# TensorE's loop over the tiles: eight steps in an iteration instead of four

## Chip, cores and metric

The kernel runs on one core of one Trainium2 chip. The metric is the device time of one execution in microseconds (us); the kernel before takes 488.36 us (median of 3 runs, 488.33 to 488.38). The engines are TensorE (PE for its matmuls, PEld for its weight loads), VectorE (DVE), ScalarE (ACT), GpSimd (POOL) and SyncE (SP). Each has a sequencer that takes instructions in the program's order, does the scalar ones (register arithmetic, branches, loads of a register) itself and hands the others to its engine.

## The reference

The input is 128 sequences of 64 tokens with 256 values each. Every sequence has two indices: one picks one of 8 experts for a first layer, the other one of 16 domains for a second.

```python
# layer 0, weights picked per sequence by expert_idx (8 experts, H = 256, I = 1024)
h = gelu(einsum('bsh,bhi->bsi', x, Wi[expert_idx]) + bi[expert_idx])
r = einsum('bsi,bih->bsh', h, Wo[expert_idx]) + bo[expert_idx] + x
y = layernorm(r) * gamma[expert_idx] + beta[expert_idx]
# layer 1, an adapter of width 64 with a matrix per domain (16 domains)
hidden = gelu(y @ down_W.T + down_b)
hidden = hidden @ expert_W[domain].T + expert_b[domain] + domain_emb[domain]
out = layernorm(hidden @ up_W.T + up_b + y) * ln_gamma + ln_beta
```

## The kernel before, in words

The host only lays arrays out. On the chip the 128 sequences are first sorted by expert, in pairs: a **tile** is two sequences, 128 tokens, and there are 64 tiles. The first 60 (PURE) have one expert each, the last 4 are mixed. Weights are kept as a high and a low half of 16 bits, so each product is three matmuls (high by high, high by low, low by high).

All engines walk through the same **steps** (`STEPS` = 69), each as a software pipeline of its own, tied to the others by semaphores alone. TensorE's `step` (line 1022) does for step i, in this order:

- the sequencer reads four words of the index table (`indices(pe, 4 * i + IDX_PE, 4, ...)`, the load is recorded at line 274): where the weights of tile i and of tile i - 1 lie and the two domains' tables. With them it works out addresses (`first_addresses`, lines 986 to 992, `second_addresses`, line 994);
- the first product of tile i, 8 columns of 6 matmuls (lines 1006 to 1008, into `p_h`), with the up product of tile i - 4 after the first column (lines 1039 and 1043, into `p_u`) and the down product of tile i - 3 after the third (line 1029, into `p_d`);
- the bias row of tile i - 1 (line 1117) and its second product, 8 times 3 matmuls (lines 1017 to 1019, into `p_o`), with the transposes of tile i - 2 in its middle (line 1051, into `p_t`).

So line 1039 occurs once in each step from step 4 on, and marks the steps in the trace.

`run` (line 288) lays the steps out on an engine: a **lead** written out in full, then a hardware loop (`eng.Fori`, line 292) whose body holds `unroll` steps, and then the rest written out. The loop's own instructions (counter, branch, start value) are recorded at line 294. For TensorE the lead is steps 0 to 5, the loop covers the 48 steps 6 to 53, and steps 54 to 68 follow, written out. `run`'s default is four steps in an iteration. GpSimd (line 562) and TensorE (line 1131) use it; ScalarE (line 693), VectorE (line 911) and SyncE (line 416) pass `NCH` = 8, because their steps name one of eight weight chunks by its place in the body. Of the chunk that `run` hands to a step, TensorE only asks whether there is one.

Of the kernel before, what the change touches and what calls it, by code (L numbers as in the profile page):

```python
# [16 lines left out]
WCH, NCH = 512, 8  # L17
# [31 lines left out]
def build(nc, t):  # L49
# [4 lines left out]
    with ctx:  # L54
# [233 lines left out]
        def run(eng, step, unroll=4, ahead=EARLY, first_looped=LEAD):  # L288

            lead, mid = first_looped - ahead, CHUNKS - FIRST_CHUNKS - ahead  # L290
            for i in range(lead):
                j = i + ahead
                step(i, i % 2, i % 4, (j % NCH, (j + FIRST_CHUNKS) // NCH, j % SLOTS_W))
            with eng.Fori(0, (mid - lead) // unroll) as n:
                i = eng.snap(n * unroll + lead)
                for q in range(unroll):
                    step(i + q, q % 2, (lead + q) % 4,
                         (q, n + (FIRST_CHUNKS + first_looped) // NCH, (first_looped + q) % SLOTS_W))
            for i in range(mid, STEPS):
                step(i, i % 2, i % 4, False)  # L300
# [121 lines left out]
        def _(pool):  # L422
# [79 lines left out]

            def step(i, parity, four, weights):
                e_third, e_before, _, _, e_next = indices(pool, i + (IDX_EXP - 3), 5, E0 - 1)
                if exists(i - 5):

# [407 lines left out]
        def _(pe):  # L914
# [213 lines left out]
                            ins.then_inc(s2_done, 1)  # L1128

            pe.wait_ge(idx_ready, TILE_READY)  # L1130
            run(pe, step)


# [45 lines left out]
```

## Time and profile before

| what | value |
|---|---|
| time, median of 3 runs | 488.36 us (488.33 to 488.38) |
| time of the profiled execution | 488.29 us |
| its span, first to last instruction | 486.5 us |
| busy: PE, PEld, DVE, ACT, POOL | 458.1, 423.3, 341.8, 362.3, 343.7 us |
| granted TensorE clock, mean | 0.98 |
| TensorE's loop, steps 6 to 53 | from about 62 to 384 us of the span |
| steps in an iteration: PE and POOL; DVE, ACT and SP | 4; 8 |

All durations of the trace come from the one profiled execution; its span is 1.8 us shorter than its own time and its time 0.07 us below the median. Times in the trace count from the span's start. PE and PEld are one engine and overlap. A row whose engine has a "q" at its end (PEldq) is of the sequencer: its time isn't counted as busy. A matmul's record begins when it begins to stream, and ends later than the next one begins; so the distance from one start to the next is what a matmul costs, not its recorded length.

### The profile page before, as it was taken

Reading aid. Unit: us, or ns where it says so; the run is one execution under the profiler, and the core shown is the slowest. Engines: PE = TensorE matmul, PEld = TensorE weight load, DVE = VectorE, ACT = ScalarE, POOL = GpSimd, SP = SyncE. Lnnn points to the kernel's source line nnn. Section 1 sums busy time; section 2 is a strip of 40 time slices with the busy share of each in tenths; the row PEclk is TensorE's granted clock in tenths of the full one; section 3 lists DMA queues with packets and bytes.
Section 4 is the critical chain, followed back from the end, with each engine's and each line's share of the span. In section 5 each row is a group of like instructions: output and inputs, shape, how many; then the busy total and the mean of one; then the engine's idle time right before and its main releaser. Section 6 shows DMA issues by size and latency. Waiting matters only on the chain.

```text
span 486.5 us, 18826 instructions
## 1 busy us (share of the span) xinstructions
PE 458.1 (94%) x5724; PEld 423.3 (87%) x5725; DVE 341.8 (70%) x910; ACT 362.3 (74%) x1087; POOL 343.7 (71%) x567
## 2 busy tenths in 40 slices
PE   3599999999999999999999999999999999999972
PEld 2388999999999999999999999999999999888861
DVE  7677777777777777777777787777777766665352
ACT  2499777887777877778877788777787777776631
POOL 5043677887778877887778877887778877754565
PEclk9889999999999999999999999999999999999995
DMA  3924334333333343433433333333332222220001
GB/s 105 333 73 106 95 99 104 104 102 92 98 100 95 103 104 87 99 96 102 104 89 95 102 101 98 86 98 101 101 98 65 60 62 61 62 56 25 26 22 34
DMA packets 66806, 44.33 MB, mean 91 GB/s; under 512 B 41537, under 2 KB 58322, under 8 KB 66642
## 3 DMA queue, kind: packets, MB, share of 16 engines
q1 hardware_dynamic: 65744, 43.68, 33.4%
q8 instruction: 18, 0.29, 0.3%
q10 hardware_dynamic: 1026, 0.21, 0.2%
q14 instruction: 18, 0.15, 0.1%
HBM read 35.47 MB, written 8.39 MB: 90 GB/s over the span
## 4 chain that ended last, share of the span: by engine, by line
PE 89%; DVE 3%; issue 2%; POOL 2%; ACT 2%; DMA 0%; POOLq 0%; DVEq 0%
PE p_o L1019 12%; PE p_o L1017 12%; PE p_o L1018 12%; PE p_h L1006 12%; PE p_h L1008 11%; PE p_h L1007 11%; PE p_d L1029 7%; PE p_u L1043 6%; PE p_t L1051 3%; PE p_u L1039 2%; PE p_o L1117 1%; PE p_h L947 1%; DVE W L810 1%; ACT h L639 0%; ACT ctab L591 0%
## 5 line engine op out<-in xcount | busy, mean ns | idle before, releaser
L1006 PE MATMUL p_h<-x_hi,W 128*128 128x128 f16 (+1 forms) x1088 | 183.5, 217 | 3.3 <-issue 3.3
L1007 PE MATMUL p_h<-x_lo,W 128*128 128x128 f16 (+1 forms) x1088 | 183.3, 217 | 0.0
L1008 PE MATMUL p_h<-x_hi,W 128*128 128x128 f16 (+1 forms) x1088 | 183.3, 217 | 0.0
L639 ACT ACTIVATE h<-p_h,bi_tile 128x128 f32<-128x128 f32 (+1 forms) x544 | 149.0, 359 | 0.0
L1018 PE MATMUL p_o<-W,h_hi 128*128 x512 | 139.6, 273 | 0.0
L1017 PE MATMUL p_o<-W,h_hi 128*128 x512 | 139.6, 273 | 0.0
L1019 PE MATMUL p_o<-W,h_lo 128*128 x512 | 139.5, 273 | 0.0
L1006 PEld LDWEIGHTS p_h<-x_hi,W 128*128 x1088 | 105.7, 98 | 9.3 <-issue 8.0
L1007 PEld LDWEIGHTS p_h<-x_lo,W 128*128 x1088 | 105.7, 98 | 1.9
L1008 PEld LDWEIGHTS p_h<-x_hi,W 128*128 x1088 | 105.6, 98 | 0.0
L539 POOL TENSOR_TENSOR rs<-mv,neg_half 128x1 f32<-128x1 f32 x64 | 55.1, 861 | 69.7 <-DVE mv L882 69.7
L665 ACT ACTIVATE a<-p_d,downb 128x128 f32<-128x128 f32 x64 | 23.5, 367 | 90.6 <-PE p_d L1029 90.6
L843 DVE SCALAR_TENSOR_TENSOR h_lo<-h,h_hi 128x512 f16<-128x512 f32 (+1 forms) x128 | 83.4, 654 | 1.9 <-ACT h_hi L650 1.8
L650 ACT ACTIVATE h_hi<-h 128x512 f16<-128x512 f32 (+1 forms) x128 | 79.1, 621 | 2.0
L551 POOL COPY sel_tile<-sel 128x128 f16 (+1 forms) x64 | 76.2, 1190 | 2.0 <-issue 2.0
L879 DVE SCALAR_TENSOR_TENSOR a1s<-a,a1s 64x128 f16<-64x128 f32 x64 | 18.5, 289 | 63.2 <-ACT a1s L668 63.1
L859 DVE SCALAR_TENSOR_TENSOR r<-p_o,x_nat 128x256 f32<-128x256 f32 x64 | 27.1, 424 | 48.1 <-PE p_o L1019 47.9
L513 POOL TENSOR_TENSOR y<-y,lng 128x256 f32<-128x256 f32 x64 | 46.5, 727 | 19.8 <-DVE h_lo L843 16.5
L686 ACT ACTIVATE yT<-p_t,gb_tile 128x128 f32<-128x128 f32 (+1 forms) x136 | 54.5, 461 | 4.2 <-PE p_t L1051 2.2
L1019 PEld LDWEIGHTS p_o<-W,h_lo 128*128 128x128 f16 x512 | 50.1, 98 | 5.8
L1018 PEld LDWEIGHTS p_o<-W,h_hi 128*128 128x128 f16 x512 | 50.1, 98 | 5.8
L1017 PEld LDWEIGHTS p_o<-W,h_hi 128*128 128x128 f16 x512 | 50.1, 98 | 4.4
(167 smaller groups left out, 825.5 us busy)
## 6 DMA issues: line engine op xcount, KB each, us to landing
stage<-in_w SPq DMA_DIRECT2D x56, 256.0 KB, 2.7
x_nat<-in_x SPq DMA_DIRECT2D x128, 64.0 KB, 2.1
out<-y SPq DMA_DIRECT2D x128, 64.0 KB, 2.0
x_T<-in_xT SPq DMA_DIRECT2D x126, 64.0 KB, 2.2
W<-in_w SPq DMA_DIRECT2D x8, 256.0 KB, 4.8
g_t<-in_gamma SPq DMA_DIRECT2D x1, 1024.0 KB, 7.0
W<-in_expert_W SPq DMA_DIRECT2D x2, 128.0 KB, 3.0
upT<-in_up_W SPq DMA_DIRECT2D x2, 64.0 KB, 2.6
```

Of the source, the lines that this page charges most:

```text
L539: pool.tensor_tensor(rs[:, 1:2], mv[:, 1, 1:2], neg_half[:, 0:1], ALU.pow).then_inc(rs2_done, 1)
L551: pool.tensor_copy(sel_tile[:, four, :].rearrange("p (n s) -> p n s", n=2), sel[:, bass.ds(2 * i, 2)].unsqueeze(2).to_broadcast([P, 2, S]))\
L639: ins = nc.scalar.activation(h[:, c, mine], p_h[parity][:, c, mine], ACT.Gelu, bias=bi_tile[:, parity, n, c:c + 1], scale=1.0 / (XS * WS))
L650: ins = nc.scalar.activation(out, h[:, cols_h, mine], ACT.Copy, scale=HS)
L686: ins = nc.scalar.activation(yT[:, k, mine], turned_z[:, mine], ACT.Identity, bias=gb_tile[:, n, KD + k:KD + k + 1], scale=gb_tile[:, n, k ...
L843: ins = v.scalar_tensor_tensor(lo[at], h[:, cols_h, mine], HS, hi[at], ALU.mult, ALU.subtract)
L1006: mm(out, hi, x_hi[:, parity, k, mine], start=(k == 0), stop=False)
L1007: mm(out, hi, x_lo[:, parity, k, mine], start=False, stop=False)
L1008: ins = mm(out, lo, x_hi[:, parity, k, mine], start=False, stop=(k == KD - 1))
L1017: mm(p_o[:, 0:D], h_high[at], hi, start=False, stop=False)
L1018: mm(p_o[:, 0:D], h_high[at], lo, start=False, stop=False)
L1019: ins = mm(p_o[:, 0:D], h_low[at], hi, start=False, stop=(j == KI - 1 and n == len(places) - 1))
```

## The change

`run` is called for TensorE with `NCH` (8) as the number of steps in an iteration. The loop still covers steps 6 to 53, now in 6 iterations of 8 steps instead of 12 of 4. The other engines' programs, the lead, the rest and every step's own work are the same.

```diff
             pe.wait_ge(idx_ready, TILE_READY)
-            run(pe, step)
+            run(pe, step, NCH)
```

## Rows read from the trace of the kernel before

**Rows 1.** The page: span, busy time, granted clock in 40 slices.
```profile
span 486.5 us, 18826 instructions
PE 458.1 (94%) x5724; PEld 423.3 (87%) x5725; DVE 341.8 (70%) x910; ACT 362.3 (74%) x1087; POOL 343.7 (71%) x567
...
PEclk9889999999999999999999999999999999999995
```

**Rows 2.** The page: shares of the chain of work that ended last, by engine.
```profile
PE 89%; DVE 3%; issue 2%; POOL 2%; ACT 2%; DMA 0%; POOLq 0%; DVEq 0%
```

**Rows 3.** Waits of PE from 384 us on: who for whom, us, times, longest.
```profile
PE p_h L1006 <- issue: 3.3, 4, 1.0
PE p_t L1051 <- DVE z L890: 1.7, 1, 1.7
```

**Rows 4.** Busy time of one loop iteration: us, engines, clock, DMA share, GB/s.
```profile
88.69:115.53 26.84, 26.84 (x338) 25.22 (x337) 19.98 (x52) 21.60 (x65) 21.59 (x33) 1.00 0.36 100
```

**Rows 5.** Timeline of PE, line 1039, steps 6, 10, 14, 18, 50, 54, 59: start, us.
```profile
62.18 0.27 PE L1039 MATMUL p_u<-parts,sel_tile 128*128 128x256 f16 x1
...
89.06 0.28 PE L1039 MATMUL p_u<-parts,sel_tile 128*128 128x256 f16 x1
...
115.90 0.28 PE L1039 MATMUL p_u<-parts,sel_tile 128*128 128x256 f16 x1
...
142.77 0.28 PE L1039 MATMUL p_u<-parts,sel_tile 128*128 128x256 f16 x1
...
357.60 0.28 PE L1039 MATMUL p_u<-parts,sel_tile 128*128 128x256 f16 x1
...
384.30 0.27 PE L1039 MATMUL p_u<-parts,sel_tile 128*128 128x256 f16 x1
...
417.67 0.27 PE L1039 MATMUL p_u<-parts,sel_tile 128*128 128x256 f16 x1
```

**Rows 6.** Timeline of PE between steps: at two iteration ends, then inside an iteration.
```profile
88.43 0.27 PE L1019 MATMUL p_o<-W,h_lo 128*128 x1
88.69 0.23 PE L1006 MATMUL p_h<-x_hi,W 128*128 128x128 f16 x1
...
115.32 0.27 PE L1019 MATMUL p_o<-W,h_lo 128*128 x1
115.53 0.23 PE L1006 MATMUL p_h<-x_hi,W 128*128 128x128 f16 x1
...
95.30 0.27 PE L1019 MATMUL p_o<-W,h_lo 128*128 x1
95.41 0.22 PE L1006 MATMUL p_h<-x_hi,W 128*128 128x128 f16 x1
```

**Rows 7.** The loop's own instructions, line 294: ns min/median/max, first and last start.
```profile
L294 PEldq FUSED_REGOPS  x12: 78/78/78, 60.0 to 355.5; - x12
...
L294 PEldq COMPARE_BRANCH  x12: 76/213/248, 86.7 to 382.1; - x12
...
L294 ACTq COMPARE_BRANCH  x6: 40/45/58, 114.5 to 383.1; - x6
```

**Rows 8.** Index loads, line 274: at an iteration's end; inside one.
```profile
L274 PEldq TENSOR_LOAD <-idx x1: 1013/1013/1013, 87.2 to 87.2; - x1
...
L274 PEldq TENSOR_LOAD <-idx x1: 1000/1000/1000, 93.6 to 93.6; - x1
```

**Rows 9.** Instruction queues: whole span; 20:60, 60:90, 385:486; 90:145. Packets, MB, share.
```profile
q8 instruction: 18, 0.29, 0.3%
...
q8 instruction: 4, 0.07, 0.7%
...
q8 instruction: 3, 0.05, 0.7%
...
q8 instruction: 11, 0.18, 0.8%
...
q14 instruction: 4, 0.03, 0.2%
```

**Rows 10.** The page, DMA issues: KB each, median us from issue to landing.
```profile
x_nat<-in_x SPq DMA_DIRECT2D x128, 64.0 KB, 2.1
```

## The prediction, made before the changed kernel ran

> **What bounds the kernel now.** I read the page first. TensorE is busy for 94% of the span at a granted clock near full speed from the first tiles to the end, and no other engine is busy for more than 74% [rows 1]; the chain of work that ended last runs over PE for 89% [rows 2]. Inside the loop this is sharper: in one iteration of 26.84 us PE is busy for all of it, while DVE, ACT and POOL have 5 to 7 us to spare [rows 4]. The list of waits of PE names nobody in the loop; what it has late in the span lies behind the loop, in the mixed tiles and the drain [rows 3]. So in the loop the time is what TensorE's own stream takes, and only a hole in that stream can be won. The list of waits is blind to short holes, because a matmul's record is longer than its place in the stream. The starts show them.
>
> **The hole.** Line 1039 stands once in each step. Behind the loop, where steps are written out, five steps take 417.67 - 384.30 = 33.37 us, 6.674 us each [rows 5]; four such steps are 26.70 us. From step 6 to step 50 (62.18 to 357.60 us, 11 iterations, 11 taken branches) it is 295.42 us, where 11 times 26.696 is 293.66: 1.76 us too much, 0.16 us for each taken branch. The last four steps, 357.60 to 384.30, take 26.70: the last branch, which falls through, costs nothing. The place of the loss is seen in the timeline: inside an iteration the first matmul of line 1006 begins 0.11 us behind the last one of line 1019, at iteration ends 0.26 and 0.21 us behind [rows 6], thus 0.15 and 0.10 us late; the rest of the loss follows in the next few matmuls.
>
> Why there: the sequencer must load four index words (1.0 us) and work addresses out before the first matmul of a step can be handed over. Inside an iteration that load begins at 93.6 us for a matmul at 95.41, 1.8 us ahead, so it is hidden behind matmuls already queued. At the iteration's end it begins at 87.2 us for a matmul that starts at 88.69, 1.45 us ahead [rows 6, 8], and there the array waits for it, so some 1.45 us is what the load and the address work need. An ordinary step has about 0.35 us of slack; the loop's end takes more. What takes it is on the sequencer: a branch of 213 ns (median; 76 ns when it falls through) and a register operation of 78 ns, with the counter's arithmetic around them [rows 7].
>
> **The change, part by part.** (1) It removes six of the eleven taken branches: 6 iterations have five taken ones and one that falls through. Nothing else on TensorE is removed; matmuls, waits, index loads and their order are the same, and 48 steps divide by 8. (2) The six that go are the first, third, fifth, ... of now. They aren't the same size as the others: the first iteration as line 1039 shows it takes 89.06 - 62.18 = 26.88 us, the second 115.90 - 89.06 = 26.84, the third 26.87 [rows 5], and so on in turn. Over 26.696 the odd ones lose 0.184 and 0.174 us, the even one 0.144. Six of the odd kind at 0.178 are 1.07 us; the five that stay hold the rest of the 1.76, 0.69 us. (3) What comes in the place of a removed end is an inner step, whose load has 0.35 us of slack: no new hole. (4) Nobody else becomes late: ACT has 5.2 us to spare in 26.84, and the ten and more steps behind the loop already run one after another at 6.674 us without a pause while the same engines feed them. (5) Behind the loop the work only moves forward by 1.07 us; its holes are TensorE's own issue and a chain through VectorE, which move with it. (6) The queues: SP's transfers are released by semaphores at the same places; 0.36 of DMA time leaves room for a step that is 0.03 us shorter.
>
> The sum, against the profiled execution: 488.29 - 1.07 = 487.22 us; the median of the runs is 0.07 above that execution, so 487.29, said as **487.3 us**, 0.22% less. A difference of about 0.2% (0.98 us) is what a measurement of this kernel can tell from no change, so this gain lies just above that edge. Bounds of the gain: if the five ends that stay cost as the odd ones do, 0.178 instead of 0.14 each, 0.20 us go back and 0.88 remain (487.5). The turn of odd and even is something whose cause I don't know, and with fewer branches it may fall either way; I take the even size because every end that stays is an even one of now. Downward, 1.2 us is as far as I go (487.1): the total of 1.76 would need the last five to vanish as well.
>
> **A branch's price.** By the trace a taken end costs the array 0.14 to 0.18 us and the sequencer a branch of 213 ns [rows 5, 7]. The Trainium skill, page "Advanced Engine Details and Errata", section "Control Flow Timing", gives about 108 ns for a compare-and-branch. By that figure, six of them would be an estimated 0.65 us, and the result 487.7; the trace has twice that for TensorE's taken branch, and half of it for ACT's, and the measurement stands.
>
> **Rival A, slower: the larger body no longer stays loaded.** The trace has queues that fetch instructions. q8 brings packets of 16 KB (0.29 MB in 18), and I take it for TensorE's: TensorE has most of the instructions, and q8 works just when TensorE runs code for the first time: 4 packets from 20 to 60 us, 3 from 60 to 90 us (the first iteration), 11 from 385 us on [rows 1, 9]. That is all 18: from 90 to 385 us there is none, so a body of four steps, which touches three to four blocks, stays at hand through all iterations. Eight steps are six to seven blocks, some 110 KB, and no row shows that seven are kept. What speaks for it: ACT, DVE and SP loop over eight steps already, and q14, which is theirs and POOL's, fetches 4 packets from 90 to 145 us and no more until 385 [rows 9]. What speaks against: theirs are far smaller bodies. If the first block is gone when the branch jumps back, the sequencer waits for it with nothing left to hide behind, since the array waits there as it is. A price for each of the five taken branches: at least a packet's own time, 0.7% of 16 engines' 30 us over 3 packets, 1.1 us; at most about what a 64 KB transfer needs from issue to landing, 2.1 us [rows 9, 10]. I take 2.1, since a fetch has to be asked for. The later blocks would come while matmuls run: a block lasts some 9 us. The time: 487.3 + 5 x 2.1 = 497.8 us, with 5 x 1.1 it is 492.8. It decides from 0.21 us a branch on (1.07 / 5): above that the gain is gone. Chance 0.16.
>
> The Trainium skill, page "Runtime: NRT & Kernel Launch", section "Instruction fetch mechanics", speaks against the change: instruction memory is two lines with sequential prefetch, and a taken branch to a target outside that window stalls for a fetch of it. By two lines of 16 KB a jump over three blocks would already fetch, and the trace shows none, so for TensorE that sentence doesn't hold. The same section gives TensorE 128 KiB, which would hold an estimated eight blocks of 16 KB, and by that this body just fits.
>
> **Rival B, no change to be seen.** The hole was never the branch's, but lies in something of every fourth or eighth step (a register reused, the index table's place), or the longer body needs more register work where its wait values are formed, so a hole opens in its middle. Then the time stays at 488.4 us, or up to 0.3 us less. Against: the branch that falls through leaves no hole though its code before and behind is that of a step, and the 11 steps written out behind the loop have none. Chance 0.05.
>
> **Rival C, the change works and gives less:** 0.8 to 0.97 us, because ends that stay take the odd size. 487.4 to 487.6 us, and within 0.2%. Chance 0.28.
>
> **How the numbers follow.** Forecast (gain 0.98 to 1.2 us) 0.51; C 0.28; B 0.05; A 0.16. Faster by over 0.2%: the forecast, 0.51. Within: B and C, 0.33. Slower: A, 0.16. The range from 487.1 to 488.5 holds the forecast, C and B, 0.84 less a little for what lies below; A is what is left out.
>
> **What would show it.** In the changed kernel's trace: 6 branches at line 294 on PEldq; first matmuls of steps 10, 18, 26, ... 0.11 us behind line 1019 as inside; two iterations of now, 53.72 us from step 6 to step 14, become 53.5; q8 has 18 packets in all, three more of them between 90 and 115 us and none from there to 384; step 54 of line 1039 at 383.2 instead of 384.3. Rival A would show as more than 18 packets on q8 and holes of a microsecond and more at 115, 169, 222 us; B as a hole of 0.1 us in the middle of the body; C as ends of 0.17 to 0.18 us where 0.14 is expected. A loss in the loop without packets on q8 would make the whole reading wrong.

## The result, and the profile after

The changed kernel takes 487.14 us (median of 11 runs, 486.63 to 487.81), where the kernel before, run beside it, takes 488.30 (11 runs, 487.96 to 488.79). The ratio is 0.9974 with a 95% interval of 0.9966 to 0.9982: 0.26% less, somewhere between 0.18 and 0.34%. Carried to the 488.36 us shown above that is 487.09 us, a hair below the low end of the range, and on the forecast's side. The two profiled executions took 488.29 and 487.38 us, 0.91 us apart.

The first lines of the page answer to [rows 1] and look the same; the shares of a page don't show a change of this size.

```profile
span 485.6 us, 18802 instructions
PE 457.4 (94%) x5724; PEld 423.8 (87%) x5725; DVE 341.8 (70%) x910; ACT 361.8 (74%) x1087; POOL 344.0 (71%) x567
```

Twenty-four instructions fewer, and none of them a matmul: on the six removed ends TensorE's sequencer saves four each. Three of the four are the loop's own at line 294 (columns as in [rows 7]); the fourth is register arithmetic of the index:

```profile
L294 PEldq FUSED_REGOPS  x6: 78/78/78, 60.0 to 327.9; - x6
L294 PEldq ALU_OP  x6: 32/32/32, 113.3 to 381.1; - x6
L294 PEldq COMPARE_BRANCH  x6: 76/213/248, 113.4 to 381.2; - x6
```

Six branches, at the same price each as before. The timeline of PE on line 1039, for steps 6, 14 and 54, answers to [rows 5]:

```profile
62.20 0.27 PE L1039 MATMUL p_u<-parts,sel_tile 128*128 128x256 f16 x1
...
115.77 0.28 PE L1039 MATMUL p_u<-parts,sel_tile 128*128 128x256 f16 x1
...
383.38 0.27 PE L1039 MATMUL p_u<-parts,sel_tile 128*128 128x256 f16 x1
```

The loop is 383.38 - 62.20 = 321.18 us long; it was 322.12. From step 54 to the end of the span it is 102.2 us in both. The reader finds the 0.94 us where they were taken out: the middle of the body (88 us) is now like any inner step, and the ends that stay (115 and 169 us) still have their hole. The timeline between the steps answers to [rows 6]:

```profile
88.45 0.27 PE L1019 MATMUL p_o<-W,h_lo 128*128 x1
88.56 0.22 PE L1006 MATMUL p_h<-x_hi,W 128*128 128x128 f16 x1
...
115.14 0.27 PE L1019 MATMUL p_o<-W,h_lo 128*128 x1
115.39 0.23 PE L1006 MATMUL p_h<-x_hi,W 128*128 128x128 f16 x1
...
168.72 0.27 PE L1019 MATMUL p_o<-W,h_lo 128*128 x1
168.94 0.23 PE L1006 MATMUL p_h<-x_hi,W 128*128 128x128 f16 x1
```

And the instruction queues, as in [rows 9]: the whole span, then 90 to 115 us, then 385 to 486 us.

```profile
q8 instruction: 20, 0.33, 0.3%
...
q8 instruction: 3, 0.05, 0.8%
...
q8 instruction: 10, 0.16, 0.7%
```

The longer body brings three packets more in its first pass, and from 115 to 385 us q8 has none: all of the body stays loaded. (The code behind the loop took 10 packets instead of 11.)

### The profile page after: what moved, and what is told of

Read it like the earlier page. It is cut to its first block, busy times and chain, and to the rows that moved or that the text cites. A ratio compares the mean times of both kernels' runs of the same rounds, so it can differ in the third digit from the quotient of the medians.

```text
span 485.6 us, 18802 instructions
## 1 busy us (share of the span) xinstructions
PE 457.4 (94%) x5724; PEld 423.8 (87%) x5725; DVE 341.8 (70%) x910; ACT 361.8 (74%) x1087; POOL 344.0 (71%) x567
## 4 chain that ended last, share of the span: by engine, by line
PE 89%; DVE 3%; issue 2%; POOL 2%; ACT 2%; DMA 0%; POOLq 0%; DVEq 0%
PE p_o L1019 12%; PE p_o L1018 12%; PE p_o L1017 12%; PE p_h L1006 12%; PE p_h L1007 11%; PE p_h L1008 11%; PE p_d L1029 7%; PE p_u L1043 6%; PE p_t L1051 3%; PE p_u L1039 2%; PE p_o L1117 1%; PE p_h L947 1%; DVE W L810 1%; ACT h L639 0%; ACT ctab L591 0%
## 5 line engine op out<-in xcount | busy, mean ns | idle before, releaser
L665 ACT ACTIVATE a<-p_d,downb 128x128 f32<-128x128 f32 x64 | 23.5, 367 | 90.2 <-PE p_d L1029 90.2
```

## The experiments

**The changed kernel again, and the kernel before again.** The first is the change itself, the second the file of before, unedited.

> The changed kernel once more, beside the three below. By the branch theory (a taken branch at the end of TensorE's loop puts the sequencer 0.5 us behind, and the array waits 0.14 to 0.19 us) the loop is 0.93 to 1.07 us shorter than before: step 6 to step 54 on line 1039 in 321.0 to 321.2 us against 322.12, and the times are 0.9 to 1.1 us under before. Rival: part of the 1.16 us between the medians came from outside the loop; then the loop again shows 0.94 and the times again 1.2 or more.

> The kernel before, once more, as a control. If the 0.2 to 0.4 us by which the times fell more than the loop did (1.16 and 1.30 us against 0.93 and 0.85) is scatter of what lies ahead of and behind the loop, this copy's loop again takes 322.1 us while its stretches before step 6 and behind step 54 differ from the first profile's by 0.1 to 0.3 us. If a taken branch costs more than the first profile showed (0.21 us by the times), the loop takes 322.6 us.

The change: 487.15 us (12 runs) against 488.45, ratio 0.9969 (0.9946 to 0.9993). Before: 488.58 against 488.52, ratio 1.0003 (0.9994 to 1.0012). Line 1039 for steps 6 and 54, of the change:

```profile
62.04 0.27 PE L1039 MATMUL p_u<-parts,sel_tile 128*128 128x256 f16 x1
...
383.31 0.27 PE L1039 MATMUL p_u<-parts,sel_tile 128*128 128x256 f16 x1
```

and of before:

```profile
62.40 0.27 PE L1039 MATMUL p_u<-parts,sel_tile 128*128 128x256 f16 x1
...
384.67 0.27 PE L1039 MATMUL p_u<-parts,sel_tile 128*128 128x256 f16 x1
```

321.27 and 322.27 us: the loop again gives back 1.0 us. In this second profile of before the eleven ends, steps 9, 13, 17 and so on to 49, last 6.82 to 6.86 us each, without the turn of large and small that [rows 5] show.

What lies outside the loop differs from one execution to the next. The kernel before reaches step 6 at 62.18 us in one profile and at 62.40 in the other. From step 54 to the end of the span it takes 102.2 us in the one and 101.7 in the other; in the drain, from 470 to 476 us, the granted clock (the number after the engines' busy times) was 0.83 in the first and 1.00 in the second:

```profile
470.00:476.00 6.00, 3.27 (x22) 2.48 (x21) 3.11 (x10) 1.97 (x6) 4.21 (x8) 0.83 0.09 22
...
470.00:476.00 6.00, 3.12 (x25) 2.29 (x23) 3.25 (x10) 1.97 (x6) 4.02 (x9) 1.00 0.09 22
```

The medians fell by 1.16 and 1.30 us, 0.2 to 0.3 more than the loop; the intervals (0.9 to 1.7 us in the first comparison) take in both, and so does the difference between executions outside the loop. Whether the rest is scatter isn't settled by these runs.

**Twelve, sixteen and twenty-four steps in an iteration.**

```diff
-            run(pe, step)
+            run(pe, step, 12)      # and 16, and 24
```

> TensorE's loop with 12 steps in an iteration (4 iterations, 3 taken branches). Branch theory alone: the loop loses 3 x 0.16 = 0.5 us, 1.3 us less than before. Instruction memory theory: the body is over 2200 instructions, nine to ten blocks of 16 KB; if eight blocks are kept, its first block is gone at each branch back: q8 then fetches in every iteration (some 36 to 45 packets in all instead of 23 for code fetched once), and each of 3 taken branches costs 1 to 2 us of holes more: 3 to 6 us, so 2 to 5 us slower than before. If it is all hidden, the first number stands and q8 still shows the packets.

> TensorE's loop with 16 steps in an iteration (3 iterations, 2 taken branches), a body of about 3050 instructions, twelve to thirteen blocks. Branch theory alone: 1.76 - 0.33 = 1.4 us less than before. Instruction memory theory: 2 taken branches with a fetch of 1 to 2 us each in the open, 0.6 to 2.6 us slower than before; q8 fetches 12 or 13 packets in each of the 3 iterations.

> 24 steps in an iteration, one taken branch. By what twelve and sixteen showed (each taken branch to code no longer kept 3.4 to 3.9 us on the sequencer, 4 to 5 us of holes in the array): 320.3 + 4 to 5 = 324.3 to 325.3 us for the loop, 2 to 3 us slower than before. If the cost goes with the number of blocks in the body and not with the branches, it is as slow as sixteen steps (7 us more than before).

Twelve: 501.25 us, ratio 1.0251 (1.0206 to 1.0296). Sixteen: 496.72, 1.0152 (1.0106 to 1.0197). Twenty-four: 493.12 in one run, before at 488.5. All of them have fewer taken branches than the change, and all are slower than before: by 12.8, 8.3 and 4.6 us, where at most 5, 2.6 and 3 us were expected. Here the branches of the loop in the kernels with twelve, sixteen and twenty-four steps:

```profile
L294 PEldq COMPARE_BRANCH  x4: 76/3543/3788, 140.0 to 394.2; - x4
```

```profile
L294 PEldq COMPARE_BRANCH  x3: 79/3548/3926, 166.7 to 389.3; - x3
```

```profile
L294 PEldq COMPARE_BRANCH  x2: 83/2047/4011, 220.2 to 386.9; - x2
```

A taken branch that took 0.21 us takes 3.4 to 4.0 us (the middle number is a median with the branch that falls through among them). In the kernel with twelve steps q8 fetches 35 packets from 118 to 385 us, where the change fetches none, 56 in all; and behind the first branch TensorE stands for 3.5 us:

```profile
q8 instruction: 56, 0.92, 0.8%
...
q8 instruction: 35, 0.57, 0.9%
```

```profile
145.55 0.23 PE L1006 MATMUL p_h<-x_hi,W 128*128 128x128 f16 x1 [3.51 <-issue]
```

The loops take 334.27, 329.35 and 326.78 us on line 1039. Over the 320.3 of a loop without a hole that is 4.7, 4.5 and 6.5 us for each taken branch. It has two parts. At every one of the six branches the array stands for 3.3 to 4.0 us. And in four of the six cases the step behind is longer too (7.9 to 8.9 us instead of 6.67), because the granted clock is lower in it. In the kernel with twelve steps this is so behind the first branch and not behind the second; the clock in these steps was 0.79 and 1.00, and within the first of them, from 148 to 150 us, it was 0.50, the lower of the two levels (1.2 GHz). TensorE had stood still from 142.0 to 145.5 us before:

```profile
145.93:154.24 8.31, 8.31 (x87) 7.90 (x85) 4.26 (x12) 5.03 (x15) 4.79 (x7) 0.79 0.30 75
...
231.01:237.69 6.68, 6.68 (x87) 6.33 (x85) 4.35 (x12) 4.62 (x15) 2.58 (x6) 1.00 0.40 97
...
148.00:150.00 2.00, 2.00 (x20) 1.94 (x19) 0.64 (x3) 1.44 (x5) 0.08 (x1) 0.50 0.62 162
```

The long steps behind the other three branches (the third of this kernel, the second of that with sixteen steps, the one of that with twenty-four) show a clock of 0.84, 0.83 and 0.74. So a taken branch costs 3.4 and 3.5 us in the two cases where the clock stays up and 5.2 to 6.5 us in the four where it falls. The cost goes with the branches, not with the length of the body. This is rival A's mechanism, at over twice the price given for it, and it begins between eight steps (six packets in the first pass, thus a body over six to seven blocks of 16 KB, all kept) and twelve (nine packets in the first pass, nine to ten blocks, not kept).

**All 48 steps in one iteration.**

```diff
-            run(pe, step)
+            run(pe, step, 48)
```

> TensorE's loop with all 48 steps in one iteration: no branch is taken. Branch theory: all 1.76 us go, 486.5 to 486.6 us where before is 488.3, and step 6 to step 54 on line 1039 takes 48 x 6.674 = 320.35 us, every step 6.67. Rival: reading 48 steps of code once from memory (about 36 packets of 16 KB more on q8) disturbs the stream; then single steps are longer than 6.68 us where packets land.

486.08 us (12 runs), ratio 0.9945 (0.9922 to 0.9969). No branch is taken, every step from 6 to 53 takes 6.67 us, and the loop 382.97 - 62.65 = 320.32 us:

```profile
62.65 0.27 PE L1039 MATMUL p_u<-parts,sel_tile 128*128 128x256 f16 x1
...
382.97 0.27 PE L1039 MATMUL p_u<-parts,sel_tile 128*128 128x256 f16 x1
```

q8 fetches 50 packets, one every 9 to 10 us, and no step is longer for it: code read once, in order, costs nothing here. The first expectation held to 0.03 us in the loop. The time is lower than it gave (486.5 to 486.6): 2.4 us under before, 0.4 to 0.6 us more than the loop gives back. The profiled execution, with 486.88 us, was the slowest of the twelve, so its trace can't say where the rest lies.

**No load at an iteration's end.** Is it the branch that holds the array up, or the branch together with the load?

```diff
+            fixed = [indices(pe, 4 * LEAD + IDX_PE, 4, DOMAIN_TOP)]    # once, ahead of the loop
...
-   zip(indices(pe, 4 * i + IDX_PE, 4, DOMAIN_TOP), ...)
+   zip(fixed[0] if first_of_iteration else indices(pe, 4 * i + IDX_PE, 4, DOMAIN_TOP), ...)
```

(`first_of_iteration`, and `last_of_iteration` further down, stand for the place of the step in the body.) The kernel leaves out the index load of each iteration's first step: all these steps work with one set of words, by the code (`4 * LEAD`) those of step 8 and not of step 6, as the expectation has it, so their tiles get wrong weights. The matmuls stay as many.

> Four steps in an iteration as before, but the first step of each iteration takes its four index words from registers that were loaded once ahead of the loop (so these tiles use step 6's weights). Theory: the hole is the sequencer's lost lead, and without the 1.0 us load it has 0.85 us to spare at an iteration's end: first matmuls 0.11 us behind line 1019 everywhere, the loop in 320.3 us, 1.7 us less than before. Rival: the branch itself holds the array up; then the holes of 0.20 to 0.25 us stay.

Twelve iterations, eleven taken branches, no hole. Behind the first branch, in the timeline (the edit moves the kernel's lines by four, so 1019 and 1006 are 1023 and 1010):

```profile
89.82 0.27 PE L1023 MATMUL p_o<-W,h_lo 128*128 x1
89.93 0.22 PE L1010 MATMUL p_h<-x_hi,W 128*128 128x128 f16 x1
```

The marker's line goes from 63.58 to 383.89 us, 320.3 us. The array never waits for the branch as such. The time, 487.85 us (ratio 0.9983, 0.9974 to 0.9992), is only 0.7 below before (488.52). The load added ahead of step 0 stands in the open: that step's own load begins at 23.5 us instead of 22.5, and step 6 comes at 63.58 us instead of 62.18.

**More work for the sequencer in inner steps.**

```diff
+                for _ in range({1: 2, 2: 6}.get(place_in_iteration, 0)):
+                    pe.sem_inc(spare, 1)
                 there, here, *domains = [ ... indices(pe, 4 * i + IDX_PE, 4, DOMAIN_TOP) ...
```

> Four steps in an iteration as before, with extra sequencer work ahead of the index load: 2 semaphore increments in the second step of each iteration, 6 in the third (some 0.1 to 0.13 us each). Theory: an inner step has 0.35 to 0.39 us of slack, so 2 (0.2 to 0.26 us) leave no hole, and 6 (0.6 to 0.78 us) leave one of 0.2 to 0.4 us: 12 of them, 2.5 to 5 us slower than before. Rival (the sequencer catches up from deeper queues, only branches hurt): no hole at either place, no change.

Two increments in the second step leave no hole (0.07 us in the first iteration), six in the third one of 0.58 to 0.66 us:

```profile
95.98 0.27 PE L1023 MATMUL p_o<-W,h_lo 128*128 x1
96.09 0.22 PE L1010 MATMUL p_h<-x_hi,W 128*128 128x128 f16 x1
...
102.65 0.27 PE L1023 MATMUL p_o<-W,h_lo 128*128 x1
103.31 0.23 PE L1010 MATMUL p_h<-x_hi,W 128*128 128x128 f16 x1 [0.39 <-issue]
```

The loop is 329.39 us long and the time 495.63 in one run, 7 us above before, where 2.5 to 5 were expected. In the trace the increments begin 0.15 us apart, so two are 0.30 us and six 0.90, and the 0.35 us of slack lie between: the threshold is where it was put, an increment only costs more than I had reckoned.

**The load taken over the branch.** If the hole is a load at a bad place, the load can move and the branch stay. The index words of the next iteration's first step are loaded in the last step (for the first iteration in step 5), into four registers kept over the branch; nothing is left out. Three places in that step were tried: ahead of the second product (carried), in its middle behind the transposes (later), and behind its first nine matmuls, so that three more stand between the load and the transposes (ahead).

```diff
+            keep = [pe.alloc_register(f"keep{n}") for n in range(4)]
...
-   zip(indices(...), ...)
+   zip([pe.snap(r, min_val=0, max_val=DOMAIN_TOP) for r in keep] if first_of_iteration else indices(...), ...)
...
                 for j in range(KI):
+                    if j == TR_AT - 1 and last_of_iteration:        # load_ahead; the others at the places named
+                        pe.load(keep, idx[0:1, bass.ds(4 * (i + 1) + IDX_PE, 4)])
                     if j == TR_AT and exists(i - 2):
                         transpose()
```

> Four steps in an iteration as before, but the index words of the next iteration's first step are loaded in the middle of the last step (ahead of its second product), into four registers that are kept over the branch. Nothing is left out. Theory: the branch's half microsecond then meets a step with no load in front of its first product, and the middle of a step has room for 1.0 us of it: no hole at 12 iteration ends, the loop in 320.3 us as without a branch, 1.7 to 2.3 us less than before, level with the loop in one iteration (486.1). Rival: the load in the middle opens a hole of its own there (a gap of over 0.11 us between two matmuls of lines 1017 to 1019 in every fourth step).

> The same with eight steps in an iteration: again 320.3 us for the loop, the same time as with four. If branches still cost something that the load had hidden, it is below four by 6 times that.

Carried: 491.81 us with four steps (1.0069, 1.0057 to 1.0081), 488.86 with eight (1.0009, 1.0001 to 1.0018). The hole at the branch is gone, and a larger one stands where the load went: in the timeline of the kernel with four steps, from the bias row (line 1122) to the second product it is 0.52 us instead of 0.11.

```profile
85.82 0.27 PE L1122 MATMUL p_o<-bo_parts,sel_tile 128*128 128x256 f16 x1
86.34 0.27 PE L1021 MATMUL p_o<-W,h_hi 128*128 x1 [0.25 <-issue]
```

The load began at 85.3 us, 0.5 us ahead of the bias row in the array. During the first product matmuls follow one another at 0.056 us, so as many of them queued would last half as long; that this is why the lead is short there is argued and not shown.

> As load_carried_four, but the load stands in the middle of the second product, behind the transposes. There, ahead of the second product, the sequencer was only 0.5 us ahead of the array and the 1.0 us load opened a hole of 0.41 us; in the second product it then gained 26 matmuls in 0.95 us where the array takes 0.11 us for each. Theory: half a second product on, its lead is 1.5 us, the load leaves 0.5 us, the remaining twelve matmuls bring it back to 1.4 us, and the branch with the address work needs 0.95 us: no hole at either place, the loop in 320.3 us, 1.8 to 2.3 us less than before (486.1 to 486.7). Rival: the lead is smaller in the middle than reckoned, a hole of 0.1 to 0.4 us stays there and the time is that of before or above.

> The same with eight steps in an iteration. By the theory the same 320.3 us as with four; if a hole of some size stays at each load, half the loss of the kernel with four.

Later: 491.04 us with four (1.0052, 1.0038 to 1.0065), 489.17 with eight (1.0013, 1.0004 to 1.0022). The theory of the expectation fell: the hole stays, now behind the transposes. What its lead had to wait for stands in two views, VectorE's timeline and the sequencer's load:

```profile
112.87 0.41 DVE L894 TENSOR_SCALAR z<-r,mv,rs 128x256 f32<-128x256 f32 x1
```

```profile
L1127 PEldq TENSOR_LOAD <-idx x2: 1002/1002/1002, 86.4 to 113.5; - x2
```

z is ready at 113.28 us, the load begins at 113.5 (113.45), and the transposes, which wait for z, run in the array only from 113.95 us on. The array doesn't wait, so no list of waits shows it; the sequencer is held until z is there. The first thing that the sequencer does behind the transposes begins 0.05 us after z's end, at every one of the loads of both kernels.

At the end of a step it isn't z that sets the lead. In the kernel before, the index loads of the 36 inner steps begin 0.38 us behind the end of z, in six of them 0.30 us behind it, and the first matmul follows the load by 1.82 or 1.83 us in all; there the lead is the same however z comes.

> Four steps in an iteration; the load for the next iteration's first step stands ahead of the transposes, behind nine matmuls of the last step's second product (one column earlier than in load_later_four). In load_later_four the load began at 113.45 us, just after VectorE had delivered z at 113.28 us, for which the transposes wait: the sequencer stood at that wait, its lead was 0.6 us, and the hole was 0.34 us. Theory: ahead of the transposes the sequencer has to stand still until z is there anyway, from about 1.0 us before, so the load is covered: no hole at any place, the loop in 320.3 us, 486.1 to 486.7. Rival (the queue's depth alone sets the lead, some 16 matmuls): the load still begins only 0.5 to 0.7 us ahead of the array and leaves a hole of 0.3 us, the time is 491 as with load_later_four.

> The same with eight steps in an iteration: by the theory 320.3 us for the loop as with four; by the rival half of four's loss, 489.

Ahead: 486.54 us with four steps (0.9965, 0.9952 to 0.9979) and 486.54 with eight (0.9958, 0.9944 to 0.9972). In the kernel with four steps the load begins at 85.2 us and ends at 86.2, where z of that step runs until 86.27; the matmul behind the load runs at 86.61 us, 1.4 us after the load's start, so the 0.5 to 0.7 us of the rival are out:

```profile
L1125 PEldq TENSOR_LOAD <-idx x1: 1003/1003/1003, 85.2 to 85.2; - x1
```

```profile
85.86 0.41 DVE L894 TENSOR_SCALAR z<-r,mv,rs 128x256 f32<-128x256 f32 x1
```

It lies in time that the sequencer had to stand still for anyway. The loop goes from 62.11 to 382.43 us, 320.32, with eleven taken branches in it, and no step from 6 to 53 is longer than 6.68 us:

```profile
62.11 0.27 PE L1043 MATMUL p_u<-parts,sel_tile 128*128 128x256 f16 x1
...
382.43 0.27 PE L1043 MATMUL p_u<-parts,sel_tile 128*128 128x256 f16 x1
```

Both kernels are shorter in the loop than the change by 0.9 us and level with the one that takes no branch. By the medians they are 0.6 us faster than the change, within what the intervals leave open, and the body of four steps stays three to four blocks of code.

## Why the prediction was right, and where it was off

**The bound and the hole**: right. All of the loop's gain is in the six ends that went; without a branch taken the loop is 320.32 us, so the hole was 1.80 us in all (1.95 in the second profile), where [rows 5] had given 1.76.

**Why there**: right, and shown from three sides. Taking the load away closes the hole with the branch in place; adding sequencer work opens one without a branch; carrying the load to a place where the sequencer stands idle closes it with nothing left out. The 0.35 us of slack stood between two increments (0.30 us) and six (0.90). The index load's 1.45 us hold too: the first matmul follows it by 1.44 to 1.46 us at all eleven ends of before, and by 1.82 or 1.83 us in all inner steps.

**Part (2), the size of the ends**: this step failed, though not by much. It took the ends that stay as of the small kind, because each of them was the second of a pair. The turn was that of one execution: the second profile of before doesn't show it, and there the ends of both kinds last 6.84 us or a little more in the mean. Nor do the ends that stay keep the small size: steps 13, 21, 29, 37 and 45 (from one start of line 1039 to the next), which hold them now, last 6.86, 6.82, 6.86, 6.81 and 6.85 us, and in the second profile all five lie at 6.85 to 6.88. So 0.86 and 0.95 us stay where 0.69 was said, and the loop gives 0.94 and 1.00 us instead of 1.07. What sets the small differences between ends is open. That is rival C's mechanism.

**The sum and its low end**: this is the step that failed. 487.3 was said and 487.14 measured, 487.09 by the ratio: a gain of 1.16 us by the medians, and by the ratio one of 1.27, which is beyond "1.2 us is as far as I go". That bound came from TensorE's holes in the loop alone, out of one profiled execution, and put everything outside the loop at nothing. The loop gave less than the forecast, 0.94 and 1.00 us. The other 0.2 to 0.3 us lie outside the loop or in executions that weren't profiled; outside the loop two executions of the kernel before differ by 0.2 us ahead of it and by 0.5 us behind it, which the bound had no room for. Whether the change moved anything there stays open: the two profiled executions of the result differ by 0.91 us, all of it in the loop. That the median lies as near to 487.3 as it does is in part luck: a loop that gave too little and a rest that gave too much.

**Part (3) to (5)**: right; no new hole in the body's middle, nobody else late. But the "ten and more steps" behind the loop at 6.674 us, and the eleven of rival B's paragraph, were misread: five steps (54 to 58) take that, as [rows 5] have it, and the next, before the mixed tiles, takes 7.38 us.

**Rival A** didn't come about at eight steps, and is real at twelve. The sign given for it, more than 18 packets on q8, was a bad one: the change has 20, because its body is longer in its first pass, and no hole. Its price was set from the landing of a 64 KB transfer (2.1 us) and is 3.4 to 4.0 us for the branch: bounds from data transfers were too low for a fetch of code. With the granted clock that falls behind it in four of six cases, which the prediction doesn't have, it is up to 6.5 us. The Trainium skill, page "Runtime: NRT & Kernel Launch", section "Instruction fetch mechanics", says that a branch to code outside the memory's window waits for a fetch. The runs agree, and its 128 KiB for TensorE fits between the six to seven blocks of 16 KB that were kept and the nine or ten that weren't; its window of two lines doesn't.

**The branch's price**: the 0.65 us for six, estimated from the Trainium skill, page "Advanced Engine Details and Errata", section "Control Flow Timing", was too small against the 0.94 to 1.00 us of the loop; the trace's was nearer.

**Rival B**: excluded by the middle of the body, which has no hole.

## What to carry to other kernels

Where an engine is busy to the last, a hardware loop's end costs the part of the sequencer's lost time that its lead doesn't cover, not what the branch takes; measure it from start to start at an iteration's end against an inner step, since the list of waits may show nothing. Fewer ends are worth that hole each, as long as the body stays in instruction memory: beyond that a taken branch here cost 3.4 to 6.5 us, twenty times the hole and more, so count the code's fetches in the trace before making a body longer. The better cure is to move the slow register load to a point where the sequencer has to wait in any case; it keeps the body short. And sizes of a tenth of a microsecond are read from two profiles of one kernel, not from one: the turn of large and small ends was gone in the second.

## What the runs showed of the hardware beyond that

- A taken branch to code no longer kept held TensorE's sequencer for 3.4 to 4.0 us, though the packets of 16 KB on q8 themselves take about 1.1 us (0.7% of 16 engines for 30 us, over three packets, [rows 9]).
- TensorE's code fetched once and in order, 50 packets in 480 us, cost no measurable time.
- After TensorE had stood for 3.5 us (142.0 to 145.5) in the kernel with twelve steps, the granted clock was 1.00 at first and 0.50 from 147 to 150 us, and 1.00 again from 151 on; that step took 8.31 us instead of 6.67.
- The sequencer's lead over the array isn't the same everywhere: 1.8 us at the end of a step, behind the matmuls of the second product, and 0.5 us ahead of that product, behind those of the first. And the wait of the transposes for VectorE's z holds back what stands behind it on the sequencer, a register load too: its address arithmetic began 0.05 us and the load 0.17 or 0.18 us after the end of z at twelve of twelve ends.
